# A decoder layer's value-product bank joins the PSUM ring as its eighth bank

## What is computed

```python
q = (x @ Wq + bq).reshape(b, lq, H, D)
k = (embeds @ Wk + bk).reshape(b, lk, H, D)
v = (embeds @ Wv + bv).reshape(b, lk, H, D)
scores = jnp.einsum('bqhd,bkhd->bhqk', q, k) * SCALE
attn = jax.nn.softmax(scores, axis=-1)
ctx = jnp.einsum('bhqk,bkhd->bqhd', attn, v).reshape(b, lq, AD)
return ctx @ Wo + bo
```

## Time and profile before

| what | value |
|---|---|
| median of 3 runs | 3068.25 us (3066.65 to 3070.2) |
| profiled execution, its own time | 3069.01 us |
| its span in the profile | 3067.2 us |
| granted TensorE clock, mean | 0.963 |
| PE, PE weight load (PEld) busy | 92%, 76% |
| DVE, POOL (GpSimd), ACT busy | 70%, 69%, 55% |
| PE's share of the chain that ended last | 89% |

### The profile page before, as it was taken

How to read it: one execution, slowest core, us unless ns; L and a number is a source line. 1 busy time by engine, 2 the same in 40 slices (tenths; PEclk the granted TensorE clock), 3 DMA queues, 4 the chain that set the end, 5 groups by cost and what they waited for, 6 DMA issues and landing times.

```text
span 3067.2 us, 83608 instructions
## 1 busy us (share of the span) xinstructions
PE 2833.7 (92%) x28504; PEld 2329.2 (76%) x28504; DVE 2158.0 (70%) x4113; ACT 1687.2 (55%) x3422; POOL 2128.3 (69%) x1708
## 2 busy tenths in 40 slices
PE   5799999999999999999999999999999999998371
PEld 3688887888888888888888888888788888886241
DVE  6777777777777777777777777777777777774104
ACT  2466665656656656656566566566565665663020
POOL 2377777777777777777777777777777777776305
PEclk9799999999999999999999999999999999998586
DMA  3100000000000000000000000000000000000022
GB/s 97 40 1 12 2 13 3 13 2 12 3 2 13 2 13 2 13 3 13 2 13 3 2 13 2 13 2 13 3 13 2 14 14 2 2 1 1 21 92 62
DMA packets 65446, 42.02 MB, mean 14 GB/s; under 512 B 6614, under 2 KB 62635, under 8 KB 65010
## 3 DMA queue, kind: packets, MB, share of 16 engines
q1 hardware_dynamic: 62962, 32.35, 3.7%
q0 software_dynamic: 2048, 3.91, 0.5%
HBM read 28.15 MB, written 8.39 MB: 12 GB/s over the span
## 4 chain that ended last, share of the span: by engine, by line
PE 89%; issue 5%; POOL 3%; DVE 1%; ACT 0%; DMA 0%; POOLq 0%; DVEq 0%; ACTq 0%
PE ps L1315 28%; PE ps L1329 23%; PE ps L1289 8%; PE ps L1278 4%; PE ps L1279 3%; PE ps L1280 3%; PE ps L1262 3%; PE ps L1263 3%; PE ps L1264 3%; PE ps L1338 2%; PE ps L1347 2%; PE ps L1269 2%; PE ps L1437 1%; PE ps L1444 1%; PE ps L1297 1%
## 5 line engine op out<-in xcount | busy, mean ns | idle before, releaser
L587 POOL TENSOR_TENSOR key_sums<-key_sums,prob_T 128x512 f32<-128x512 f32 (+1 forms) x1408 | 1811.7, 1287 | 120.8 <-ACT prob_T L749 3.8
L977 DVE TENSOR_REDUCE mx<-ps 128x1 f32<-128x400 f32 (+1 forms) x2048 | 1077.0, 569 | 507.7 <-PE ps L1289 467.2
L749 ACT ACTIVATE prob_T<-ps 128x512 f32<-128x512 f32 x1536 | 834.1, 596 | 232.0 <-PE ps L1315 214.0
L1329 PE MATMUL ps<-prob_T,v_sb 128*64 128x256 f32 (+1 forms) x6656 | 742.4, 380 | 0.9 <-ACT prob_T L752 0.9
L1329 PEld LDWEIGHTS ps<-prob_T,v_sb 128*64 128x64 f32 (+1 forms) x6656 | 479.7, 137 | 242.1 <-issue 3.6
L583 POOL TENSOR_TENSOR key_sums<-prob_T 128x512 f32<-128x512 f32 x128 | 164.8, 1288 | 564.2 <-PE ps L1315 451.8
L1315 PE MATMUL ps<-shift,shift_w 64*128 64x256 f32 (+1 forms) x3328 | 509.5, 300 | 0.1
L1315 PE MATMUL ps<-q_hi,k_hi 64*128 64x256 f32 (+1 forms) x3328 | 476.6, 280 | 0.0
L1315 PE MATMUL ps<-q_lo,k_hi 64*128 64x256 f32 (+1 forms) x3328 | 475.1, 279 | 0.0
L1315 PE MATMUL ps<-q_hi,k_lo 64*128 64x256 f32 (+1 forms) x3328 | 473.7, 278 | 0.0
L738 ACT COPY heads_raw<-ps 128x256 f32<-128x256 f32 x128 | 47.7, 372 | 672.9 <-PE ps L1329 672.9
(11 more groups left out here) (173 smaller groups left out, 3600.0 us busy)
## 6 DMA issues: line engine op xcount, KB each, us to landing
ctx_raw<-in_ctx_dram SPq DMA_DIRECT2D x16, 768.0 KB
tables<-in_L_ffn_W_dram SPq DMA_DIRECT2D x16, 256.0 KB, 3.7
slots_in<-zeros SPq DMA_DIRECT2D x32, 64.0 KB
xs<-in_x_dram SPq DMA_DIRECT2D x8, 256.0 KB, 3.1
xres<-in_x_dram SPq DMA_DIRECT2D x8, 256.0 KB, 2.9
v_sb<-slots_in SPq DMA_DIRECT2D x8, 256.0 KB, 2.7
slots_out<-v_sb SPq DMA_DIRECT2D x8, 256.0 KB, 4.0
out_dram<-x1s SPq DMA_DIRECT2D x8, 256.0 KB, 2.4
```

The lines of the kernel that those rows point to most:

```text
L587: op = nc.gpsimd.tensor_tensor(acc[0:rows, :, :], acc[0:rows, :, :], prob_T[0:rows, :, k, :], ALU.add)
L749: nc.scalar.activation(prob_T[:, h, 2 * i:2 * i + 2, :].rearrange("p k t -> p (k t)"), ps[:, bank, :], ACT.Exp).then_inc(ring_act, 1)
L977: v.tensor_reduce(mx[:, qt, h, c:c + 1], ps[:, at.bank("mx", r, c, qt, h), 0:WID[c]], AX.X, ALU.max).then_inc(ring_dve, 1)
L1329: last = mm(ps[h * DH:h * DH + DH, HEADS, 0:T], v_sb[0:rows, r % NJ // 2 % 2, k, v0 + h * DH:v0 + h * DH + DH], prob_T[0:rows, h, k, :], s ...
```

## The change

Bank 7 becomes the eighth bank of the ring, and the value product is entered in `FILLS` as the last product of its pair, behind the denominators. The order of the products on PE is what it was, and so is the work on every engine. Three things follow. Each product now waits for the holder eight places back. The value product takes whichever bank is next, waits for its holder as the others do, and is emptied by a `ring_act` count. And the products of M and S count two new semaphores, `rows_full0` and `rows_full1`, one for each head; all others count `ring_full`, so `pv_ok` and `heads_free` go.

Counting back eight places, S(i) waits for both exponentials of S(i-2) alone, M(i) for both maxima of M(i-2) alone, the first V for the first exponential of S5. S1 waits for the copy of the pair before (`heads_out`), since its second bank is that of `attend`. A middle batch now has 337 products (before: 329), and 337 is 42 times 8 and 1: where the ring closes from batch to batch, M0 of a middle batch gets the very bank of the `attend` just ahead of it; in the last batch S0 does.

```diff
@@ -41,8 +41,7 @@
 
 
 
-RING = (0, 1, 2, 3, 4, 5, 6)
-HEADS = 7
+RING = (0, 1, 2, 3, 4, 5, 6, 7)
 SLOTS_A_BATCH = 8
 V_FILLS = 7
 
@@ -51,6 +50,14 @@
 MAX_UNITS = ((0, 0), (0, 1), (1, 0), (1, 1), (2, 0), (2, 1), (3, 0), (3, 1))
 
 UNITS = 7
+
+
+
+MAKERS = ("rows0", "rows1", "all")
+
+
+def maker(key):
+    return f"rows{key[-1]}" if key[0] in ("s", "mx") else "all"
 
 
 def value_fills(s):
@@ -112,6 +119,7 @@
                 put("dve", "ctx", 8, c)
         if s > 0 or kind != "first":
             put("act", "den", s - 1)
+        put("act", "pv", s)
     return fills
 
 
@@ -121,8 +129,9 @@
 
 
 def owned(kind, upto=None):
-    owners = [o for _, o in FILLS[kind][:upto]]
-    return {"full": len(owners), "act": owners.count("act"), "dve": owners.count("dve")}
+    fills = FILLS[kind][:upto]
+    owners, makers = [o for _, o in fills], [maker(key) for key, _ in fills]
+    return {"act": owners.count("act"), "dve": owners.count("dve"), **{m: makers.count(m) for m in MAKERS}}
 
 
 def bank_at(kind, place):
@@ -136,7 +145,7 @@
     def __init__(self, kind, b, batches):
         self.kind, self.b = kind, b
         self.start = {}
-        for of in ("full", "act", "dve"):
+        for of in ("act", "dve", *MAKERS):
             n_start, n_first, n_mid = (owned(k)[of] for k in ("start", "first", "mid"))
             if kind == "start":
                 self.start[of] = 0
@@ -168,7 +177,7 @@
         return self.start[of] + (here if own else here - owned(self._kind(own))[of])
 
     def full(self, *key):
-        return self._count("full", *self.find(*key))
+        return self._count(maker(key), *self.find(*key))
 
     def freed(self, *key):
         own, place = self.find(*key)
@@ -177,6 +186,11 @@
 
     def bank(self, *key):
         return bank_at(self.kind, PLACE[self.kind][key])
+
+    def place_of(self, *key):
+
+        own, place = self.find(*key)
+        return bank_at(self._kind(own), place)
 
     def held_by(self, *key):
 
@@ -400,12 +414,11 @@
         kh_ok = sem("kh_ok")
         qh_ok = sem("qh_ok")
         ring_full = sem("ring_full")
+        rows_full = [sem(f"rows_full{h}") for h in range(2)]
         ring_act = sem("ring_act")
         ring_dve = sem("ring_dve")
         nm_ok = sem("nm_ok")
         nspread_ok = sem("nspread_ok")
-        pv_ok = sem("pv_ok")
-        heads_free = sem("heads_free")
         rden_ok = sem("rden_ok")
         norm_ok = sem("norm_ok")
         key_sum = sem("key_sum")
@@ -716,7 +729,8 @@
                 act.wait_ge(ring_full, at.full("v", g, n))
                 if n == 0 and at.kind != "start":
 
-                    wait(act, pv_ok, at.n(1, 2 * g - 3, 1))
+                    if at.kind != "first" or g > 1:
+                        act.wait_ge(ring_full, at.full("pv", 2 * g - 3))
                 src = ps[:, at.bank("v", g, n), :].rearrange("p (k n) -> p k n", n=2 * P)
                 if n < V_FILLS - 1:
                     copy(v_sb[:, g % 2, 2 * n:2 * n + 2, :], src).then_inc(ring_act, 1)
@@ -734,16 +748,16 @@
 
             def heads_out(at, r):
                 wait(act, norm_ok, at.n(1, r, 0))
-                act.wait_ge(pv_ok, at.n(1, r, 1))
-                copy(heads_raw[:, :], ps[:, HEADS, 0:T]).then_inc(heads_free, 1)
+                act.wait_ge(ring_full, at.full("pv", r))
+                copy(heads_raw[:, :], ps[:, at.place_of("pv", r), 0:T]).then_inc(ring_act, 1)
 
             def exps(at, s, i):
-                if i == 0:
-
-                    wait(act, pv_ok, at.n(1, s, 0))
+                if i == 0 and (at.kind != "first" or s > 0):
+
+                    act.wait_ge(ring_full, at.full("pv", s - 1))
                 wait(act, key_sum, at.n(12, s - 1, min(2 * i + 1, 12)))
                 for h in range(2):
-                    act.wait_ge(ring_full, at.full("s", s, i, h))
+                    act.wait_ge(rows_full[h], at.full("s", s, i, h))
                     bank = at.bank("s", s, i, h)
                     if i < UNITS - 1:
                         nc.scalar.activation(prob_T[:, h, 2 * i:2 * i + 2, :].rearrange("p k t -> p (k t)"),
@@ -973,7 +987,7 @@
             def maxima(at, r, units):
                 for c, qt in units:
                     for h in range(2):
-                        dve.wait_ge(ring_full, at.full("mx", r, c, qt, h))
+                        dve.wait_ge(rows_full[h], at.full("mx", r, c, qt, h))
                         v.tensor_reduce(mx[:, qt, h, c:c + 1], ps[:, at.bank("mx", r, c, qt, h), 0:WID[c]],
                                         AX.X, ALU.max).then_inc(ring_dve, 1)
 
@@ -996,7 +1010,8 @@
 
             def normalise(at, r):
                 dve.wait_ge(rden_ok, at.n(1, r, 1))
-                dve.wait_ge(heads_free, at.n(1, r, 1))
+                _, count = at.freed("pv", r)
+                dve.wait_ge(ring_act, count)
                 if r == 0 and at.kind != "first":
 
                     dve.wait_ge(ring_full, at.full("out", -1))
@@ -1287,7 +1302,7 @@
                 for h in range(2):
                     lanes = slice(h * DH, h * DH + DH)
                     mm(ps[:, banks[h], 0:WID[c]], q_hi[r % 2][lanes, qt * P:qt * P + P],
-                       k_hi[r % 2][lanes, KEY0[c]:KEY0[c] + WID[c]], start=True, stop=True).then_inc(ring_full, 1)
+                       k_hi[r % 2][lanes, KEY0[c]:KEY0[c] + WID[c]], start=True, stop=True).then_inc(rows_full[h], 1)
 
             def row_shift(at, r):
 
@@ -1315,21 +1330,19 @@
                             last = mm(ps[0:rows, banks[h], n * T:n * T + T], keys_part, query_part[lanes, :],
                                       start=(step == 0), stop=(step == 3))
                             if step == 3 and k == tiles[-1]:
-                                last.then_inc(ring_full, 1)
+                                last.then_inc(rows_full[h], 1)
 
             def attend(at, r):
-                wait(pe, heads_free, at.n(1, r, 0))
-
-                _, count = at.freed("s", r, UNITS - 1, 1)
-                pe.wait_ge(ring_act, count)
+
+                bank, = banks_of(at, ("pv", r), also=[("s", r, UNITS - 1, 1)])
                 v0 = r % NJ % 2 * P
                 for k in range(KT):
                     rows = P if k < KT - 1 else KREM
                     for h in range(2):
-                        last = mm(ps[h * DH:h * DH + DH, HEADS, 0:T],
+                        last = mm(ps[h * DH:h * DH + DH, bank, 0:T],
                                   v_sb[0:rows, r % NJ // 2 % 2, k, v0 + h * DH:v0 + h * DH + DH],
                                   prob_T[0:rows, h, k, :], start=(k == 0), stop=(k == KT - 1))
-                last.then_inc(pv_ok, 1)
+                last.then_inc(ring_full, 1)
 
             def denominators(at, r):
                 pe.wait_ge(key_sum, at.n(12, r, 12))
```

## The result

The changed kernel takes **3014.26 us** (median of 4 runs, 3013.75 to 3014.42); the kernel before, timed beside it, 3067.77 (3066.65 to 3070.2). The ratio is 0.9826 with a 95% interval of 0.9812 to 0.984: 53.5 us less. The prediction said 3010, within 2996 to 3040. The profiled executions stand at spans of 3067.2 and 3011.9 us, 55.3 apart; the sum of the prediction had 58.6.

A forecast was written before the change was run, and what follows sets the result against it. PE was taken to bound the kernel, so only its gaps waiting for a bank could close. The sum: 3069.0 - 30.2 - 5.9 - 23.5 + 1 = 3010.4, 3009.6 against the median, stated as 3010, range 2996 to 3040.

The forecast's parts named there:

- What bounds the kernel: PE, busy 92% of the span with 89% of the chain; only gaps that are waits for a bank can close.
- Part 1: M7 and first V, freed from later exponentials of S5, start sooner: 30.2 us in middle batches, 5.9 in first and last.
- V stays behind M7 (3026): Rival: the switch of shapes sets the 0.41 from M7 to V, so only M7's gain counts; 3026 us, chance 0.08.
- Part 2: S2, S4, S6 wake 0.07 sooner each, a register operation and a wait behind ACT's going: 23.5 us in middle batches.
- Only the banks: Rival: the register operation costs nothing of itself, so the sooner wakes of S2, S4, S6 give 0; 3034 us, chance 0.10.
- more: Rival: at S2, S4, S6 the next weights load in time, so 0.10 each goes too, 33.6 us more; 2977, chance 0.05.
- M7 is held by PE's own stream: Rival: M7's instructions are not ready sooner and nearness to ACT's end is chance; 3046 us, chance 0.06.
- the next wait takes it: Rival: DVE's row shift or POOL's sums hold PE instead; within 0.2% of before, chance 0.05.
- Part 3, the value bank's waits: Waits for the heads' copy: M0 at loop entry 0.6, S0 in last batch 0.3, elsewhere nothing; together +1 us.
- Part 4: Signals, split of ring_full and longer look-back cost nothing; DVE and POOL should keep up with shorter pairs.
- A sign that was wrong: Expected in the changed kernel's profile: the row "PEld V waits for ACT", 27.8 us before, gone from the waits.

The follow-up runs named there:

- e5: Changed kernel, but M7 waits again also for ACT's first exponential of S5, with the wait for DVE behind it: 3054.92 us.
- e1: Kernel before, ring of 7, with two waits exchanged so that PE waits for DVE first and ACT last: 3050.33 us.
- e9: e2's kernel with 32 wait instructions, long satisfied, put once ahead of PE's loop: 3042.23 us.
- e8: Changed kernel, but M0 of each pair, not only at a batch's start, waits for the copy of the heads before it: 3088.15 us.
- e6: Changed kernel, but all products count ring_full again instead of one semaphore for each head; ring of 8 kept: 3014.49 us.
- e7: Changed kernel, but PE waits for a K chunk only at the first of its two M units and for the queries only at M0: 3007.1 us.
- e4: Changed kernel, but only the first V waits again also for the second exponential of S5: 3055.63 us.
- e2: Changed kernel, but S1 to S6 wait again for DVE's first maximum of the M before, long done, behind the wait for ACT: 3077.13 us.
- e10: Changed kernel with 32 satisfied wait instructions put once ahead of PE's loop: 3043.27 us.
- e11: Changed kernel with 16 satisfied wait instructions put once ahead of PE's loop: 3019.8 us.
- e3: Changed kernel, but M7 waits also for the first exponential of S5 and the first V also for the second: 3058.43 us.
- e12: e7's kernel with 16 satisfied wait instructions put ahead of PE's loop: 3006.22 us.

## Why the prediction was right, point by point

- **What bounds the kernel.** Right: PE still holds 89% of the chain, and all that was won is gaps between its products. DVE and POOL rose to 72% and 71% and hold nothing new.
- **Part 1, M7 and V** (35.1 measured of 36.1 in the sum: 30.2 + 5.9). M7 -0.12 (said 0.14), V -0.14 (said 0.13); in the first batch 0.84 to 0.52 and 0.38 to 0.27 (said 0.32 and 0.10). The reading that M7 was held by ACT at 0.13, although the view called it "issue", is shown by e5: give it the wait back and 114.3 us stand there again.
- **V stays behind M7 (3026)** fell: V kept 0.28, not 0.41. The page "TensorE: Matmul & The Clock Gate", Part 3, "The mechanism", of the Trainium skill would have V's load wait for M7. The trace has that load at 1483.69, 0.07 ahead of M7's modelled end, so it does not tell whether there is such a wait; M to S takes 0.18 in the same pair (1476.77 to 1476.95) and M7 to V 0.27, which leaves some 0.1 for the switch of shapes, and not the 0.41. That it is the switch is argued by this difference: no run isolates it.
- **Part 2, the wakes** (24.6 of 23.5). Each 0.07, as said. e1 shows it by an edit of one line, e9 undoes it by itself. That the three add up held: from M0 to S6 the median went from 7.58 to 7.35, 0.22 less. *Only the banks* (3034) fell with it, and *more* (2977) too: at 0.06 behind ACT the weights still come late, 1478.10 to 1478.33.
- **M7 is held by PE's own stream** and **the next wait takes it** fell: M7 follows at 0.13, and no new wait on DVE or POOL appears.
- **Part 3, the value bank's waits** (-0.9 of -1). Entry 0.62 (said 0.6), last batch 0.31 (said 0.3), none at the 13 restarts, nothing at S1. e8 measured what the stretch that covers them is worth: 0.62 a time.
- **Part 4, "No cost"**, is the step that was short. It priced counters (e6: right), DVE and POOL (right), and asked nothing of the loop as code. The change takes 3124 instructions out of the run (83608 to 80484), 1542 of them on PE, and PE's loop now begins 100 instructions sooner in its stream; the units behind a restart lost 13.0 us instead of 7.8. These 5.2 are more than the whole difference between the sum and the spans (3.3). Some 3.5 of them are stops in S1, which the last section ties to the place; the rest is mainly one spell more, which one profile cannot tell from chance. e7 got 6.9 back.
- **A sign that was wrong.** V's row in the waits did not vanish. I had taken the row's name for its cause. The gap in that row is now, by the difference above, the switch of shapes, and it carries ACT's name since ACT signalled last. It has to be read by the time between the named instruction's end and the start: 0.05 is a wait, 0.22 is not.

One thing was right in the sum and not stated: the parts are **not independent**. Each was worked out with the other in place. Alone, part 2 gives 15 us (e1) and not 23.5, since V's wait takes 0.07 of the 0.21 back; and half of part 1 gives almost nothing (e4, e5).

## What to carry to other kernels

Where an engine waits for several things, put the wait that is released last behind all others, and its register arithmetic ahead of it: one line did that here for 15 us, without a bank. When a ring is re-dealt, look at two neighbours that wait for about the same moment, for only freeing both gives anything, and put the new bank's wait one unit behind the place where it is in the open. After any edit to a loop, compare the first units behind its restart as well as the middle of it; a difference of up to 1% there says nothing about the edit.

## What the runs showed that was not expected

**The place of a loop in the instruction stream.** The same loop of the changed kernel, moved by 32 instructions, loses 45.2 us behind its starts instead of 13.0, and e2's loop, moved by the same number, 15.5 instead of 45.9: up to 35 us either way, over half of what the change itself brought. PE stops inside a unit, between products with no wait between them: 0.42 in the changed kernel, 2.19 in e2.

The traces say more on where and when. Count PE's records in the order of time, two for each product (its weight load and itself) and one for each wait or register operation. On the first turn of the loop M0 is number 4302 in the changed kernel. The product that comes late on later turns is then number 4377 or 4378 in each of the nine kernels that stop inside a unit, although it is the tenth of the 16 of S0 in e2, the first of M1 in e10, the sixth of S1 in e11, its tenth in e3 and e5 and its fourteenth in the changed kernel, e4, e6 and e8. In the kernel before and e1 (M0 is 4402) and in e9 (4381) that place lies ahead of the loop, and nothing stops inside its units. In e7 and e12 it lies in S2, which PE reaches later, a median 3.4 and 2.9 us behind M0; in the nine it comes 2.6 to 2.9 behind.

PE's instruction supply can be seen too. From the page of the changed kernel, a DMA queue (number of transfers, MB, share):

```profile
q8 instruction: 266, 4.36, 0.6%
```

Its transfers are of 16384 bytes, 17 in each turn of the loop. At every one of the 13 restarts of all 14 kernels one of them starts 2.7 to 3.4 us ahead of M0, and M0 comes 1.8 to 2.1 behind its end; the next one starts 0.1 to 0.9 behind M0 and takes 0.9 to 1.4. In the nine kernels the late product never comes less than 1.2 behind the end of that second transfer, and where it was held by more than 0.55 us (64 restarts) it comes 1.2 to 1.7 behind. So both the pause at a restart and the stop inside a unit go with instructions that arrive late, and what counts is how soon PE reaches the place from which they are missing: the nearer to M0, the longer the stop (S0 in e2, M1 in e10, S1 in the others). Fewer instructions in the loop are then not needed for a small loss (6.1 and 5.4 in e7 and e12); a place far enough behind M0, or ahead of the loop, will do. No run chose a place by this count and tested it, and the stops ahead of V in some restarts of e2, e3, e5 and e11 (0.6 to 2.1) are not explained by it.

**Spells at half clock behind a restart.** The windows of e10 behind a restart, with PE's granted clock in the column PEclk:

```profile
2478.80:2481.40 2.60, 1.85 (x18) 1.54 (x18) 1.05 (x2) 0.71 (x2) 0.00 (x0) 0.65 0.02 6
2481.40:2483.90 2.50, 2.44 (x20) 2.45 (x22) 1.06 (x2) 0.37 (x2) 1.27 (x1) 0.50 0.03 7
2483.90:2486.50 2.60, 2.60 (x26) 2.60 (x26) 1.28 (x3) 1.65 (x4) 1.29 (x1) 0.52 0.00 0
2486.50:2489.00 2.50, 2.50 (x42) 2.37 (x42) 2.23 (x5) 2.14 (x6) 2.41 (x2) 1.00 0.00 0
```

and PE's timeline in the first of them:

```profile
2478.81 0.45 PE L1304 MATMUL ps<-k_hi,q_hi 64*128 64x400 f32 x2 [1.86 <-issue]
...
2479.48 0.33 PE L1330 MATMUL ps<-q_hi,k_lo 64*128 64x256 f32 x2
2479.60 0.43 PE L1330 MATMUL ps<-shift,shift_w 64*128 64x256 f32 x2
2479.81 0.43 PE L1330 MATMUL ps<-q_hi,k_hi 64*128 64x256 f32 x2
...
2480.24 0.43 PE L1330 MATMUL ps<-q_hi,k_lo 64*128 64x256 f32 x2
2481.46 0.70 PE L1304 MATMUL ps<-k_hi,q_hi 64*128 64x400 f32 x2 [0.79 <-issue]
```

PE had idled 1.86 us; from 2479.60 on the products stand 0.21 apart and not 0.12, at a granted 0.50, the lower of the clock's two levels (1.2 GHz and not 2.4), and a unit of scores takes 1.71, not 0.95. From 2486.50 on the clock is back. Where nothing else holds PE, such a spell costs about 1.4 us, and it follows some restarts and not others: 5 of 13 before, 6 in the changed kernel, 3 in e1, 4 in e7, 8 in e11, 11 in e9, 12 in e10, all 13 in e2. The 15.5 us of e9 are nearly all spells. PE's idle time ahead of M0 does not decide it alone, as two restarts of the kernel before show. Timeline of PE, then the windows 1.5 us behind each M0, with the granted clock in the column PEclk:

```profile
2158.96 0.45 PE L1289 MATMUL ps<-k_hi,q_hi 64*128 64x400 f32 x2 [2.16 <-issue]
...
2326.81 0.45 PE L1289 MATMUL ps<-k_hi,q_hi 64*128 64x400 f32 x2 [1.55 <-issue]
...
2160.50:2162.00 1.50, 1.50 (x24) 1.29 (x22) 1.28 (x3) 1.46 (x3) 0.36 (x1) 1.00 0.00 0
...
2328.30:2330.00 1.70, 1.70 (x18) 1.70 (x18) 1.09 (x3) 1.08 (x2) 0.42 (x1) 0.50 0.00 0
```

The longer idle time kept the full clock, the shorter lost it. What decides was not found. Each count is of one profiled execution, so one spell more or less between two kernels (1.4 us) is no property of either; that e2 and e10, with the longest stops, have a spell at nearly every restart is more than that, but so has e9, which has no stops.
